# A chunked gated recurrence on one core: the cross sums between a leaf's halves by one block-diagonal product per batch, on rows that are moved on chip

## The reference, cut to what matters

```
def step(St, inp):
    kt, qt, vt, at, bt = inp
    Sk = jnp.einsum('bhij,bhj->bhi', St, kt)
    err = Sk - vt
    Sn = at[..., None] * St - (bt[..., None] * err)[..., None] * kt[:, :, None, :]
    ot = jnp.einsum('bhij,bhj->bhi', Sn, qt)
    return (Sn, ot)
...
_, outs = jax.lax.scan(step, S0, (tfirst(k), tfirst(q), tfirst(v), tfirst(a), beta.transpose(1, 0, 2)))
```

## Time and profile before

| | us |
|---|---|
| median of 3 runs | 3104.63 (3102.82 to 3107.32) |
| the profiled execution, its own time | 3104.89 |
| its span in the profile | 3103.2 |
| recurrence, first to last leaf | about 680 to 1981 |
| VectorE busy in the program | 2236.9 (72%) |
| TensorE busy in the program | 2082.5 (67%) |
| ScalarE busy in the program | 1171.3 (38%) |
| GpSimd busy in the program | 771.9 (25%) |

### The profile page before, as it was taken

How to read it: one execution, slowest core, us unless ns; L and a number is a source line. 1 busy time by engine, 2 the same in 40 slices (tenths; PEclk the granted TensorE clock), 3 DMA queues, 4 the chain that set the end, 5 groups by cost and what they waited for, 6 DMA issues and landing times. The chain is left out here.

```text
span 3103.2 us, 43267 instructions
## 1 busy us (share of the span) xinstructions
PE 2082.5 (67%) x12498; PEld 1444.2 (47%) x12498; DVE 2236.9 (72%) x5902; ACT 1171.3 (38%) x2868; POOL 771.9 (25%) x692
## 2 busy tenths in 40 slices
PE   8999999955666656565554554599968472379800
PEld 4555555524555544444443344488843341157600
DVE  5878778779999999999999997665628483023344
ACT  2555555534555555555443344433300110122200
POOL 1444444430000000000000000044435117411165
PEclk8999999977777777777666677799989565679955
DMA  2333343442566778889999992423221502049732
GB/s 94 119 120 119 119 122 119 120 135 65 142 161 165 181 179 206 207 221 232 243 261 237 274 275 60 139 66 106 79 79 24 200 29 79 3 120 270 226 98 85
DMA packets 528648, 448.37 MB, mean 144 GB/s; under 512 B 142095, under 2 KB 476734, under 8 KB 522184
## 3 DMA queue, kind: packets, MB, share of 16 engines
q1 hardware_dynamic: 422059, 314.96, 37.6%
q0 software_dynamic: 26784, 87.09, 9.3%
q10 hardware_dynamic: 79616, 44.06, 4.9%
HBM read 244.49 MB, written 207.77 MB: 146 GB/s over the span
## 5 line engine op out<-in xcount | busy, mean ns | idle before, releaser
L561 DVE SCALAR_TENSOR_TENSOR p_zo<-p_w,p_gd,p_zo 128x128 f32<-128x128 f32 x2304 | 648.9, 345 | 11.3
L384 DVE SCALAR_TENSOR_TENSOR p_y<-p_ps_proj,p_w,p_y 128x508 f32<-128x508 f32 (+2 forms) x576 | 415.8, 740 | 117.4 <-ACT p_y L298 103.8
L863 PE MATMUL p_ps_z<-p_turned,p_gcol 112*32 112x128 f32 x3584 | 229.0, 417 | 399.9 <-DMA p_turned<-history 395.7
L863 PEld LDWEIGHTS p_ps_z<-p_turned,p_gcol 112*32 112x32 f32 x3584 | 141.0, 160 | 484.2 <-issue 298.1
L846 PE MATMUL p_ps_x<-p_w,p_diag_o 128*128 128x128 f32 x2048 | 303.2, 296 | 65.3 <-ACT p_diag_o L884 25.0
L234 PE MATMUL p_ps_proj<-p_x,p_w 128*128 128x512 f32 x768 | 342.3, 596 | 2.7 <-ACT p_beta_t L289 2.7
L884 ACT ACTIVATE p_diag_o<-p_ident,p_gd 128x128 f32<-128x128 f32 x1024 | 314.3, 388 | 59.3 <-PE p_ps_x L846 53.0
L846 PEld LDWEIGHTS p_ps_x<-p_w,p_diag_o 128*128 128x128 f32 x2048 | 260.1, 200 | 108.4 <-ACT p_diag_o L884 67.0
L828 PE MATMUL p_ps_x<-p_w,p_diag_z 128*128 128x128 f32 x1536 | 215.1, 300 | 94.3 <-DVEq L581 43.1
L706 POOL DMA_DIRECT2D p_dec<-decays x32 | 17.4, 543 | 1049.4 <-DVEq L665 778.0
L897 ACT ACTIVATE p_diag_z<-p_ident,p_gd 128x128 f32<-128x128 f32 x768 | 232.6, 388 | 94.3 <-PE p_ps_x L828 76.8
(11 more groups left out here) (213 smaller groups left out, 3326.3 us busy)
## 6 DMA issues: line engine op xcount, KB each, us to landing
history<-p_hist SPq DMA_DIRECT2D x18, 2048.0 KB, 14.3
gram<-p_gram SPq DMA_DIRECT2D x64, 512.0 KB, 3.3
history_sums<-p_sums ACTq DMA_DIRECT2D x112, 256.0 KB, 6.0
p_zo<-history_sums SPq DMA_DIRECT2D x28, 1024.0 KB, 8.1
p_wgu<-in_wguT SPq DMA_DIRECT2D x64, 352.0 KB
decays<-p_dec SPq DMA_DIRECT2D x64, 256.0 KB, 2.3
beta_v<-p_bv SPq DMA_DIRECT2D x64, 256.0 KB, 2.4
p_dec<-decays POOLq DMA_DIRECT2D x32, 512.0 KB, 6.0
```

Of the source, the lines that this page charges most:

```text
L384: nc.vector.scalar_tensor_tensor(out=yv[:, :, s:], in0=pv[:, :, 0:T - s], scalar=par[j % 2][:, kind, TAPS - 1 - s:TAPS - s], in1=yv[:, :, ...
L561: return done(nc.vector.scalar_tensor_tensor(out=acc, in0=row, scalar=scalar, in1=acc, op0=ALU.mult, op1=ALU.add))
L863: last = nc.tensor.matmul(ps_z[k % NZ][h * 2 * C:(h + 1) * 2 * C, u % UB * QUADS + q, :], gcol[u % NTURN][:, q * 4 + h, :], turned[u % NTU ...
```

## The change

- The diagonal blocks go, with everything that makes and uses them: diagonals_o, diagonal_z, cross_z, cross_o.
- VectorE's share of the cross sums goes too (rows 6 and 7 of z), and the five z fills become two, of four late steps each (128x512).
- The early rows of a leaf are moved, SBUF to SBUF, by 8 DMAs on GpSimd's queue (send_rows): batch b's 16 partitions of 8 rows become near_w[:, b, :], with (head, row) on 128 partitions.
- The gram values of (early row, late step) are loaded by 32 DMAs per leaf (load_near) into the block-diagonal tile near_g: per batch 128 partitions (head, row) by 256 columns (z or o, head, late step). Off-diagonal blocks are zero from one clearing at the start. These loads of the next leaf are issued as soon as this leaf's products are done.
- One product per batch (near) gives all z and o cross sums of its 16 heads, with the width on partitions: 8 products of 128x128 by 128x256, in pairs, through two PSUM tiles ps_n. ScalarE copies each pair (near_rows, 4 copies of 128x512) to near_t, and 16 transposes of 128x128 on TensorE bring them into ps_x, sequences on partitions again. Four transposes make a fill.
- On TensorE near(next leaf) stands behind the 16 units of history products, where cross_z stood; on ScalarE near_rows stands behind the 8 batch_rows.
- To make room, ps_z and sums have 2 buffers in place of 4 (NZ, NS).
- On GpSimd the 8 row moves stand first after half_done, ahead of the next decays and the store of the outputs; the 32 gram loads stand behind the store and ahead of the wait for leaf_done.

```diff
-    NZ = 4
+    NZ = 2
...
-        NS = 4
+        NS = 2
...
+        near_w = m.sb("p2_near_w", [P, BG, DH])
+        near_g = m.sb("p2_near_g", [P, BG, 2, H, HALF])
+        near_t = m.sb("p2_near_t", [DH, 2, BG, H, HALF])
...
-        Z_FILLS = ((0, 1), (1, 2), (2, 4), (4, 6), (6, 8))
-        O_FILLS = ((0, 4), (4, 8))
+        Z_FILLS = ((0, 4), (4, 8))
...
-                for f, rows in ((0, range(RZ, HALF)), (1, range(RO, HALF))):
-                    for r in rows:
-                        after(h_at)
-                        for k in range(HALF):
-                            h_at = add_scaled(zo[g][:, f, HALF + k, :], w[g][:, 1 + r, :],
-                                              gd[g][:, r, f * C + HALF + k:f * C + HALF + k + 1])
...
+            def send_rows(at):
+                g = at % GR
+                pool.wait_ge(half_done, at + 1)
+                if at:
+                    pool.wait_ge(near_mm, at * PAIRS)
+                for b in range(BG):
+                    pool.dma_start(near_w[:, b, :], w[g][b * H:(b + 1) * H, 1:1 + HALF, :]).then_inc(near_in[b // (BG // 2)], DMA)
+            def load_near(c, g):
+                at = c * GR + g
+                if at:
+                    pool.wait_ge(near_mm, at * PAIRS)
+                for h in range(H):
+                    for f in range(2):
+                        e0 = c * 2 * C + f * C + HALF
+                        pool.dma_start(near_g[h * HALF:(h + 1) * HALF, :, f, h, :],
+                                       gram_dram[g * BG:(g + 1) * BG, h, c * C:c * C + HALF, e0:e0 + HALF]
+                                       .rearrange("b r e -> r b e")).then_inc(near_g_in, DMA)
...
+                    send_rows(at)
                     if at + 1 < LEAVES:
-                        pool.wait_ge(half_done, at + 1)
                         load_half(*following(c, g), 0)
                     if at:
                         store_o(at - 1)
+                    if at + 1 < LEAVES:
+                        load_near(*following(c, g))
...
+            def near(c, g):
+                at = c * GR + g
+                first = isinstance(c, int) and at == 0
+                pe.wait_ge(near_g_in, at * (2 * H * DMA) + 2 * H * DMA)
+                for k in range(PAIRS):
+                    if k % 2 == 0:
+                        pe.wait_ge(near_in[k // 2], at * (BG // 2 * DMA) + BG // 2 * DMA)
+                    pe.wait_ge(near_cp, at * PAIRS + k + 1)
+                    for j in range(2):
+                        b = k * 2 + j
+                        last = nc.tensor.matmul(ps_n[k % NN][:, j, :], near_w[:, b, :],
+                                                near_g[:, b].rearrange("p f h e -> p (f h e)"), start=True, stop=True)
+                    last.then_inc(near_mm, 1)
+                pe.wait_ge(near_cp, at * PAIRS + PAIRS + NN)
+                for f in range(2):
...
+                    turn = near_t[:, f].rearrange("p b h e -> p (b h) e")
+                    for e in range(HALF):
+                        ins = nc.tensor.transpose(ps_x[:, f * 2 + e // 4, e % 4, :], turn[:, :, e], ident[:])
+                        if e % 4 == 3:
+                            ins.then_inc(x_done, 1)
...
+            def near_rows(c, g):
+                at = c * GR + g
+                if at:
+                    act.wait_ge(x_done, at * FILLS)
+                for k in range(PAIRS):
+                    act.wait_ge(near_mm, at * PAIRS + k + 1)
+                    nc.scalar.copy(near_t[:, :, 2 * k:2 * k + 2].rearrange("p f b h e -> p f b (h e)"),
+                                   ps_n[k % NN][:].rearrange("p b (f x) -> p f b x", f=2)).then_inc(near_cp, 1)
```

More of the change, by code:

```diff
@@ L486, in recurrence @@
         leaf_done = m.sem("p2_leaf_done")
[L487 to L490, removed]
+        near_in = [m.sem(f"p2_near_in{i}") for i in range(2)]
+        near_g_in = m.sem("p2_near_g_in")
+        near_mm = m.sem("p2_near_mm")
+        near_cp = m.sem("p2_near_cp")
         x_done = m.sem("p2_x_done")
@@ L633, in leaf @@
                                                 in0=zo[g][:, 0, HALF + k0:HALF + k1, :],
-                                                in1=ps_x[:, (fill - 1) % 4, 0:k1 - k0, :], op=ALU.add).then_inc(step_done, 1)
+                                                in1=ps_x[:, fill - 1], op=ALU.add).then_inc(step_done, 1)
                         after(z_at)
@@ L747, in _ @@
                             pool.wait_ge(kept[g], (c + 1) * 2)
-                        pool.wait_ge(diag_o_used, (at + 1) * DUNITS + NDO)
+                        for i in range(2):
+                            pool.wait_ge(near_in[i], (at + 1) * (BG // 2) * DMA)
                         load_gram(c + 1, g)
@@ L753, in _ @@
             for i in range(NS):
-                pool.wait_ge(z_out[i], GR * ROUNDS * 2 * DMA)
+                pool.wait_ge(z_out[i], GR * ROUNDS * (BG // NS) * DMA)
         @block.sync
@@ L805, in _ @@
                         for i in range(NS):
-                            sp.wait_ge(z_out[i], (at * 2 + half + 1) * DMA)
+                            sp.wait_ge(z_out[i], (at * (BG // NS) + (half + 1) * (ZB // NS)) * DMA)
                         sp.dma_start(zo[g][seqs].rearrange("p f s i -> p (f s) i"), sums_dram[g, seqs]).then_inc(zo_in[g], DMA)
@@ L810, in _ @@
         def _(pe):
[L811 to L843, removed]
-                            for e in range(DO):
-                                r = q * DO + e
-                                last = nc.tensor.matmul(ps_x[:, O_BANK + j, k - k0, :], diag_o[u % NDO][:, e, :],
-                                                        w[g][:, 1 + r, :], start=(r == 0), stop=(r == RO - 1))
-                            last.then_inc(diag_o_used, 1)
-                            u += 1
-                    pe.wait_ge(diag_o_used, at + u + NDO)
-                    pe.sem_inc(x_done, 1)
@@ L853, in _ @@
-            cross_z(0, 0)
+            pe.wait_ge(cleared, 2 * NTURN + 3)
+            def near(c, g):
[13 more added lines that the diff above has]
+                for f in range(2):
+                    if not first:
+                        if f == 0:
+                            pe.wait_ge(x_z_read, at * len(Z_FILLS))
+                        else:
+                            pe.wait_ge(o_seen, at)
+                    turn = near_t[:, f].rearrange("p b h e -> p (b h) e")
[3 more added lines that the diff above has]
+                            ins.then_inc(x_done, 1)
@@ L930, in _ @@
                         batch_row(c, g, b)
-                    for u in range(NDZ, DUNITS):
-                        diagonal_z(*following(c, g), u)
-            diagonals_o(NCHUNK - 1, 0)
-            for u in range(DUNITS):
-                diagonal_z(NCHUNK - 1, 1, u)
-            diagonals_o(NCHUNK - 1, 1)
+                    near_rows(*following(c, g))
+            near_rows(NCHUNK - 1, 1)
         used = m.sems
```

63 lines of the change are left out of this document (17 added, 46 removed).

## The result

| | before | after |
|---|---|---|
| median, us (6 runs each) | 3104.15 (3102.13 to 3107.32) | 3117.93 (3113.07 to 3120.96) |
| ratio | | 1.0043, 95% interval 1.0031 to 1.0056 |
| span of the profiled execution, us | 3103.2 | 3119.3 |
| end of leaf 15 in the profile, us | 1981.0 | 1988.9 |

Slower by 0.43%, 13.8 us. The forecast was 3123, 18 us more; range 3080 to 3168. The profiled execution is itself 3.0 us above the median of the changed kernel's runs.

A forecast was written before the change was run, and what follows sets the result against it. VectorE was taken to set the recurrence's pace, with TensorE's freedom nearly the limit from leaf 9. Terms: +24.1 first fills, +1.8 leaves 0 and 15, -14 fills, -12 later waits, +18 DMA: +18, so 3123 us; range 3080 to 3168.

The forecast's parts named there:

- The pace and the place: In the recurrence VectorE sets the pace; the wait that could replace its saving is at each leaf's first fill.
- The first fill's shift: Leaves 1 to 14: VectorE's 4.5 us saving against the new chain less today's gap, together +24.1 us.
- a later TensorE through DMA: Moved rows, 0.52 MB a leaf, delay the history loads and so TensorE's freedom: 1.7 us in late leaves, 18 us in all.
- The chain N: From TensorE free with operands to the first fill, through products, last copy and four transposes: 7.5 us, against about 3.1 before.
- Leaves 0 and 15: Leaves without history units: first fill at half + 13.5 in place of half + 12.6, losing 0.9 us each, +1.8.
- Fills and later waits: On VectorE, two fills for five gain 0.9 us a leaf, 14 us; later fills no longer wait, 12 us.
- The row moves' landing: Each 64 KB row move on GpSimd's queue lands in 4 us, bounds 2.2 and 6.0.
- Queues, buffers, gram loads: GpSimd's added issues, halved history-sum buffers and small gram loads were each taken as costing nothing.
- The signs: What the trace would show if right, including idle time ahead of the first fill, 3 to 6 us in late leaves.
- The short chain: Rival: chain of 5.0 us and no DMA price, so VectorE's saving shows; 3075 us, chance 0.24.
- Two buffers: Rival: halved buffers throttle the history products, TensorE freed 3 us later in 14 leaves; +42, 3165 us, chance 0.13.
- Late issues: Rival: GpSimd's row-move issues sit out VectorE operations, rows land some 10 us later; 47 us more, 3170, chance 0.05.

The follow-up runs named there:

- e3: Changed kernel with the row moves of all leaves but the first left out, products reading leaf 0's rows: 0.9999 of the kernel before.
- e1: Kernel before with two PSUM and two SBUF buffers for the history sums in place of four, nothing else: 1.0004 of the kernel before.
- e4: Changed kernel without the 32 gram loads of all leaves but the first, leaf 0's values used throughout: 1.0039 of the kernel before.
- e9: Changed kernel with z's products, copies and transposes ahead of o's, and the chain after the 12th history unit: 0.9844 of the kernel before.
- e10: Changed kernel with z ahead of o, chain after the 12th unit, and SyncE's history writes ahead of its history-sums wait: 0.9783 of the kernel before.
- e11: Kernel before with SyncE's history writes put ahead of its wait for the history sums: 1.0003 of the kernel before.
- e12: Changed kernel, chain behind the last unit, with SyncE's history writes ahead of its wait for the history sums: 1.0018 of the kernel before.
- e8: Changed kernel with z of all batches first, in products of 128 columns, then o: 0.9968 of the kernel before.
- e5: Kernel before with VectorE's 16 operations of the cross sums left out, cross_z and all else kept: 0.9919 of the kernel before.

## Why the prediction was right, step by step

*The pace and the place.* Right. What VectorE no longer does came back as idle time ahead of the fills. That the idle time in the stretch of the earlier trace rows grew by 86 us, just what was promised (72 + 14), is chance: VectorE's busy time fell by 72 us in the recurrence, not by 86.

*The first fill's shift.* The prediction's sum was +24.1 for leaves 1 to 14, and +18 for a later TensorE through DMA: 42. Read from both traces in the same way it is +27.6. Two terms were too large:
- The chain N is 7.0 us as a mean over the leaves that wait (6.3 to 7.8), not 7.5. That is 0.5 in some 13 leaves, 6 us. The 8 products take 5.4 us as a mean, as forecast (5.5); the last copy takes 0.76 where 0.9 was put, and the four transposes 0.8 where 1.1 was.
- The chain begins 9 us later, summed over leaves 1 to 14 (from +3.1 to -4.1 in a leaf), not 18. I had let the moved 0.52 MB push everything else back at the rate of a full DMA. How much of the 9 us is theirs stays open: e3's time gives the moves some 10 us in these leaves, give or take 5, but in its trace the last units come as late without them, and e1's come 6 us later in sum with the halved buffers alone, which is no more than two executions differ by. That the DMA had room is not it: while leaf 9's rows are moved, from 1402 to 1408 us, the share is 1.14.

*Leaves 0 and 15.* +1.8 forecast. Against the half, leaf 15's first fill came 0.6 us earlier. Leaf 0's came 1.8 later (721.0 against 719.2, the half at the same time): +1.2 together.

*Fills and later waits.* -26 forecast, -21 found; with the two items above that makes the recurrence's +7.8. The later waits went, 12 us. A leaf without them runs from first fill to end in 32.6 us, where it had been 33.1: a fill saved 0.5 us a leaf in place of 0.9. The step that failed here counted each removed fill's whole step of 0.44 or 0.57 us. VectorE's queue around one of them in leaf 9, first in the kernel before and then in the changed one:

```profile
1448.76 0.82 DVE L558 TENSOR_TENSOR p_w<-p_w,p_dec 128x640 f32<-128x640 f32 x1
1449.49 0.41 DVE L632 TENSOR_TENSOR p_zo<-p_zo,p_ps_x 128x256 f32<-128x256 f32 x1
1450.05 0.49 DVE L558 TENSOR_TENSOR p_zo<-p_zo,p_pp 128x128 f32<-128x128 f32 x2
```
```profile
1447.80 0.82 DVE L556 TENSOR_TENSOR p_w<-p_w,p_dec 128x640 f32<-128x640 f32 x1
1448.65 0.49 DVE L556 TENSOR_TENSOR p_zo<-p_zo,p_pp 128x128 f32<-128x128 f32 x2
```

From the operation ahead to the addition behind, 1.29 us became 0.85. That saves 0.44 where the fill's own step was 0.56, since the fill started 0.73 us after the operation ahead and the addition now starts 0.85 after it. Three fills less, at 0.12 each, are 0.36 of the missing 0.4.

*The row moves' landing.* Taken as 4 us, found 2.2 to 7.5, median 4.9. In leaf 15 the products begin 4.1 us behind the half, while the last of the 8 moves are being issued (forecast: 6), and the fill comes at half + 12.2, forecast 13.5.

*Queues, buffers, gram loads.* All three taken as nothing: e4 shows it for the loads, e1 for the buffers, the issue times of lines 720 and 730 for GpSimd. The clearing of near_g, taken as nothing too, cost leaf 0 about 2 us.

*The signs.* The prediction named idle time of 3 to 6 us ahead of the first fill in late leaves. Its own sum says more: 4.5 us freed and a fill 4.4 us later make 9. Found were 5.4 to 11.5 us in leaves 6 to 13, and 26.6 in leaf 14, which had 14.2 before.

*The sum's remainder.* The recurrence ends 7.8 us later in the profile, and the span is 16.1 longer. Of the other 8.3, 3.4 us lie between the issue of the last store of outputs and the next stage's first instruction (8.0 before, 11.5 after). The rest is in stages that the change doesn't touch. All that follows leaf 15 takes 1122 us before and 1130 after; in the other profiled kernels, e9 and e10 left out, it takes 1118 to 1128. A steadier figure comes from three traces of each recurrence, from the first step of leaf 0 to the last of leaf 15: 1293.7, 1297.5 and 1294.8 us in the kernel before, e1 and e11; 1303.5, 1305.0 and 1304.1 in the changed kernel, e4 and e12. That is 9 us more, where the sum said 18. The other 4 or 5 of the measured 13.8 lie outside the recurrence, are not explained, and had no term in my sum. So the mechanism and the sign were right, the recurrence's loss was put at twice its size, and that 18 is as near 13.8 as it is owes something to luck.

*The rivals.* The short chain did not happen, but e8 shows how near it was: 1.7 us less chain turns the sign. Its break-even was put at N = 6 with the DMA price; e8, at 5.3, is 10 us faster than before. Two buffers: e1 excludes the 42 us. Late issues: issue times exclude it. The Trainium skill's rule on the shared port (SBUF — State Buffer, A bandwidth-pool intuition that's wrong) speaks of a VectorE copy, and I had set it against issues beside VectorE's sums, mostly no copies; so those rows say little about it. A fairer look is at the 15 copies of 128x128 (L647) that stood beside issues of gram loads: they took 219 to 221 ns, and no issue of that line over 637 ns. The most that shows beside an issue is 0.08 us: in the kernel before, 11 of the 15 copies at the start of a leaf, beside issues of L706, took 0.30 us in place of 0.22. A wait of the kind did appear elsewhere, between VectorE's first copy and GpSimd's clearings.

## What to carry to other kernels

When an engine's queue is thinned, look first at what it waits for next and by how little: here the supplier began only 3 to 5.5 us ahead of the fill in nine leaves, and its shortest way to the fill took 3.1, so even without the new chain (e5) a saving of 4.5 us was in large part turned into waits. A batched form with less work in all, but a chain of stages (move, product, copy, transpose) that delivers its first result only when all is done, has to be placed earlier in the supplier's queue than the form it replaces; behind the 12th unit it is worth 1.4%, behind the 8th 0.8%; that the earlier place starves the loads behind it fits the rows, but was not tried by itself. And once a leaf is shorter, the queue orders that had been harmless become the next bound: SyncE's was worth nothing in the kernel before and 0.6% in the fast one.

## What was not expected of the hardware

Transposes whose weights are read with a step of 8 elements have the longer weight load, 189 ns as a median against 140 for the contiguous ones of the earlier trace rows, but 16 of them take 2.04 us, where 8 contiguous ones took 1.33, both at a granted clock of 1.00; without the last one's 0.27 us that is 0.12 us apiece against 0.15.

```profile
L854 PEld LDWEIGHTS p_ps_x<-p_ident,p_near_t x256: 185/189/209, 720.2 to 1957.1; 128*128 128x128 f32 x128
```

So the price of 0.7 us a leaf that a rule of the Trainium skill (SBUF — State Buffer, Door 1: The DMA port swizzle) would have added did not come: the load is longer by a third, and the stream of transposes is no slower.
